# Audio tower kernel: part of the attention beside the last scans, scans and loads reordered, unread products on TensorE

## The chip, the cores and the metric

The kernel runs on one NeuronCore of a Trainium2 chip. The core has five engines that each work through their own list of instructions in order and wait for each other through semaphores: PE (TensorE, matrix products), DVE (VectorE), ACT (ScalarE), POOL (GpSimd) and SP (SyncE, which here only issues DMA transfers). The metric is the device time of one launch in microseconds. The three timed runs of the kernel before took 843.44, 845.51 and 848.17 us, median 845.51 us. The profiled execution took 837.19 us, of which its span is 835.0 us.

## The reference, cut to what matters

The reference has three parts in a row: three state-space layers with a halving of the sequence between them (750, 375, 187 positions), an attention with polynomial features, and a mixture of 16 experts. All is in 32-bit floats.

```python
def _ssm_layer(x, A_log, Dp, W_dbc, W_dt, b_dt):
    A = -jnp.exp(A_log)
    dbc = jnp.einsum('ble,ce->blc', x, W_dbc)
    delta, Bm, Cm = jnp.split(dbc, [DT_RANK, DT_RANK + N_STATE], axis=-1)
    delta = jax.nn.softplus(jnp.einsum('blr,er->ble', delta, W_dt) + b_dt)
    dA = jnp.exp(delta[..., None] * A)
    dBx = (delta * x)[..., None] * Bm[:, :, None, :]
    _, hs = jax.lax.associative_scan(combine, (dA, dBx), axis=1)
    return jnp.einsum('blen,bln->ble', hs, Cm) + Dp * x
# between layers: x.reshape(b, l // 2, 2, d).mean(axis=2)

h = h + attention(_layernorm(h))   # qkv, q and k divided by their norms, products of features, y / y_norm, projection
h = h + ffn(_layernorm(h))         # gate, softmax, the best 2 of 16 experts, silu(h1) * h2, w3
```

## The kernel before, in words

The batch of 32 is laid out as 2 groups of 64 channels on 128 partitions, 16 sequences in a row on the free axis. The scans are cut into 28 *units*: 16 of 750 columns for the first layer, 8 for the second and 4 for the third. Units are gathered in eight *phases* (`PHASES`: six of 4 units, then two of 2; `UB` holds where each begins). `LAST` is 26, the first unit of the last phase; unit 27 (`LAST + 1`) ends the scans. For each phase a short chain of dependent steps decides from the extremes of the step sizes which of the 64 states are slow: `extremes`, `extremes_of_row`, `lowest`, `bounds`, `smallest_delta`, `exponents`, `classes`, `ranked_and_quadratic`, `picks`. The two slowest states (`STATIC`) are scanned one by one; the others decay at once and are done by a product of the matrices (`mixed`, `product`, `summed`, `by_delta`, `output`). If a phase has more slow states, `more_slots` loops over them; with this data the loops are branched over.

For one unit n the work is this.

- PE: `rows` makes the rows of C and of the step size; `mixed` and `summed` serve the fast states; `weighted_b(n, j)` makes the input of scan j; `sums(n, part)` adds neighbouring positions for the next layer.
- SP: `spread_rows` takes these rows through a buffer in DRAM and spreads each over 64 partitions (`St`, the step size, and `Ct`, C). `EVENTS` lists which rows belong together: event k holds C of one unit and the step size of the unit two later; `ROWS` says in which period each is made.
- ACT: `softplus` (the step size), `decay` (the factors of the scan), `rows_out` and `sums_out` (copies out of PSUM).
- POOL: `softplus`, `inputs` (step size times x) and `add` (which puts the unit's result in its place).
- DVE: `load`, `recur` (the scan, 1.7 us for a unit), `read` for both states; `product`, `by_delta`, `output`.

Every engine has a function `period(n)` which writes its instructions out in a fixed order, and the periods -2 to 27 follow one another. Nothing else sets the order: an instruction that waits holds up all that is behind it on its engine. In period n DVE scans unit n and prepares unit n + 1; PE prepares n + 1 and n + 2. `chain(n)` gives q, the place in a phase of four at which steps of the next phase's decision are woven in; `brief(n)` gives k = 0 and 1 for the periods 24 and 25, in which the last phase's decision is woven in between a phase of only two units; `straight(n)` marks the first decision, before any scan.

After the scans comes `attention()`, a pipeline over eight parts r of 376 columns (`QC`) in periods t. `stages(t)` gives the part that is in each stage: the first layernorm (`first_center`, `first_squares`, `first_variance`, `first_deviation`, `first_normalized`), then qkv and its norms (`project_qkv`, `qkv_bias`, `qk_squares`, `qk_sums`, `qk_norms`, `qk_scale`, `k_linear`, `q_linear`), then the features (`products`, eight multiplications each, on POOL for k and mostly for q, on DVE for q of part 0) and `moments`, `q_features`, `attend`, and so on. In the kernel before t = 0 and t = 1, in which only the first two stages have work, begin when unit 27 is done. Then `experts()` follows, bound by PE.

At the start SP loads x in seven parts (`X_PARTS`): four of one unit each, then three of 1500 KB. The 15 small weights of attention and experts (`later`) are issued in one go behind event 4.

## Time and profile before

| what | us |
|---|---|
| median of three timed runs | 845.51 |
| profiled execution | 837.19 |
| its span | 835.0 |
| start, to the first product of the scans at | 29.17 |
| scans end, first product of attention at | 370.06 |
| first `moments` product of attention at | 397.05 |
| experts, first product at | 559.17 |

The page's line of the clock over the span in 40 slices shows the two places at which TensorE was slow: `PEclk9989999999999997666999999999999999999999`. The line of GB/s below it shows the loads at the left. To read this table: what happens before 29 us is a serial chain; from there to 315 us DVE and PE are both busy in most slices, with a few lower ones among them; between 315 and 397 us, where the last phases are short and the attention starts, every engine waits for others; from 397 us on a pipeline runs evenly, and from 559 us on PE never waits.

### The profile page before, as it was taken

How to read it: one execution, taken by the hardware profiler on the slowest of the kernel's cores; microseconds unless marked ns; L12 is line 12 of the kernel's file. 1: busy time of each engine (PE TensorE's matmuls, PEld its weight loads, DVE VectorE, ACT ScalarE, POOL GpSimd, SP SyncE). 2: the span in 40 equal slices, each digit the busy share in tenths (PEclk: the TensorE clock that was granted, in tenths of full speed). 3: DMA queues.
4: the chain of work that ended last, by engine and by line, in shares of the span. 5: the costliest groups of instructions: out<-in, count | busy, mean ns of one | idle time of the engine just before them, and what ended most of it. 6: DMA issues, size and time to landing. Idle time of an engine off the chain costs nothing.

```text
span 835.0 us, 11071 instructions
## 1 busy us (share of the span) xinstructions
PE 728.1 (87%) x3474; PEld 360.5 (43%) x3474; DVE 549.6 (66%) x859; ACT 426.2 (51%) x761; POOL 440.1 (53%) x402
## 2 busy tenths in 40 slices
PE   5778898989899894745998888878999999999997
PEld 2334444545445452412776666742333333333332
DVE  3477899998889896475458888849354444454443
ACT  2767587868676873512354554443334433344332
POOL 1457668686868575723555555523344444443441
PEclk9989999999999997666999999999999999999999
DMA  3475443424344432132000000072584443444400
GB/s 129 139 225 154 105 120 91 133 80 113 94 114 112 112 96 76 37 88 52 2 1 1 3 3 4 3 147 59 122 178 95 90 88 85 89 100 99 105 1 19
DMA packets 29233, 70.19 MB, mean 84 GB/s; under 512 B 4387, under 2 KB 20079, under 8 KB 28527
## 3 DMA queue, kind: packets, MB, share of 16 engines
q1 hardware_dynamic: 28863, 68.77, 33.7%
q8 instruction: 31, 0.51, 0.3%
q10 hardware_dynamic: 304, 0.63, 0.2%
q14 instruction: 35, 0.29, 0.1%
HBM read 66.96 MB, written 2.43 MB: 83 GB/s over the span
## 4 chain that ended last, share of the span: by engine, by line
PE 44%; DVE 8%; ACT 2%; issue 1%; DVEq 0%; ACTq 0%
PE pair L818 21%; PE pair L839 11%; PE pair L721 4%; PE pair L704 3%; PE pair L753 2%; DVE big L1420 1%; PE pair L768 1%; PE pair L740 1%; PE pair L762 1%; PE pair L685 1%; DVE big L1425 0%; ACT big L1100 0%; DVE big L1438 0%; DVE big L1728 0%; DVE big L1475 0%
## 5 line engine op out<-in xcount | busy, mean ns | idle before, releaser
L1583 DVE TENSOR_TENSOR hidden<-pair,tmp 128x502 f32<-128x502 f32 (+1 forms) x192 | 121.6, 675 | 129.4 <-PE pair L818 104.9
L1702 POOL TENSOR_TENSOR hidden<-xs,big 128x502 f32<-128x502 f32 (+1 forms) x96 | 111.9, 1167 | 167.4 <-PE pair L818 146.8
L1153 ACT ACTIVATE tmp<-pair 128x502 f32<-128x502 f32 (+1 forms) x192 | 102.5, 586 | 157.2 <-PE pair L818 157.2
L1728 POOL TENSOR_TENSOR big<-big 94x512 f32<-94x512 f32 (+3 forms) x120 | 89.7, 781 | 78.0 <-DVE big L1485 71.2
L818 PE MATMUL pair<-xs,w 64*128 64x502 f32 (+1 forms) x384 | 107.4, 636 | 0.5 <-DVE big L1517 0.5
L818 PE MATMUL pair<-hidden,w 64*128 64x502 f32 (+1 forms) x384 | 98.3, 588 | 3.1 <-DVE hidden L1583 3.0
L1293 DVE TENSOR_TENSOR_SCAN pair<-tmp,pair 128x750 f32<-128x750 f32 (+1 forms) x56 | 95.9, 1713 | 0.3
L839 PE MATMUL pair<-hidden,w 128*64 128x502 f32 (+1 forms) x384 | 91.1, 596 | 0.0
L463 PE MATMUL pair<-big,work 128*128 128x512 f32 x112 | 65.6, 669 | 7.6 <-DVE work L1305 4.3
L1605 POOL TENSOR_TENSOR big<-big,work 128x750 f32<-128x750 f32 (+1 forms) x28 | 45.6, 1629 | 46.9 <-ACT big L896 46.6
L818 PEld LDWEIGHTS pair<-hidden,w 64*128 64x128 f32 x384 | 37.0, 188 | 49.8 <-issue 44.8
L818 PEld LDWEIGHTS pair<-xs,w 64*128 64x128 f32 x384 | 29.4, 186 | 67.3 <-issue 36.2
L1633 POOL TENSOR_TENSOR big<-big,work 128x375 f32<-128x375 f32 (+1 forms) x24 | 22.0, 917 | 66.9 <-ACT big L964 66.5
L1286 DVE TENSOR_TENSOR pair<-pair,big 128x750 f32<-128x750 f32 (+1 forms) x56 | 52.0, 929 | 5.5 <-PE pair L464 5.0
L913 ACT ACTIVATE tmp<-big,picked 128x749 f32<-128x749 f32 (+2 forms) x56 | 49.9, 910 | 7.5 <-POOL big L1610 5.3
L839 PEld LDWEIGHTS pair<-hidden,w 128*64 128x64 f32 x384 | 23.4, 136 | 61.9 <-DVE hidden L1583 34.8
L1615 POOL TENSOR_TENSOR big<-big 128x750 f32<-128x750 f32 (+1 forms) x28 | 46.7, 1667 | 2.2
L1610 POOL TENSOR_TENSOR big<-big,work 128x750 f32<-128x750 f32 (+1 forms) x28 | 46.2, 1650 | 2.2
L1608 POOL TENSOR_TENSOR work<-work 128x750 f32<-128x750 f32 (+1 forms) x28 | 46.1, 1648 | 1.3 <-ACT work L902 1.3
L721 PEld LDWEIGHTS pair<-big 93*120 93x120 f32 (+1 forms) x384 | 42.1, 184 | 2.6 <-issue 1.4
L721 PE MATMUL pair<-big 93*120 93x65 f32 (+1 forms) x384 | 42.6, 268 | 0.0
L1271 DVE TENSOR_TENSOR pair<-pair,big 128x750 f32<-128x750 f32 (+1 forms) x28 | 26.4, 944 | 22.3 <-PE pair L464 16.7
(185 smaller groups left out, 1281.4 us busy)
## 6 DMA issues: line engine op xcount, KB each, us to landing
big<-dispatched SPq DMA_DIRECT2D x40, 502.0 KB, 6.6
spread<-rowsd SPq DMA_DIRECT2D x48, 375.0 KB, 5.7
spread<-rowsd SPq DMA_DIRECT2D x48, 187.5 KB, 3.3
big<-in_x SPq DMA_DIRECT2D x3, 1500.0 KB, 9.3
big<-dispatched SPq DMA_DIRECT2D x8, 498.0 KB, 5.8
spread<-rowsd SPq DMA_DIRECT2D x8, 374.0 KB, 4.9
w<-in_w SPq DMA_DIRECT2D x5, 512.0 KB, 7.0
big<-in_x SPq DMA_DIRECT2D x4, 375.0 KB, 3.8
```

The costliest lines, as they stand in the source:

```text
L463: pe.matmul(dst[:, 0:512], lhsT, rhs[:, 0:512], start=True, stop=True)
L721: mm = pe.matmul(bank[4 + n % 2][0:FT, at:at + 65], kF[r % 2][0:rows, unit, FT * f:FT * f + FT], qkv[r % 2][0:rows, unit, 143:208], start= ...
L818: pe.matmul(dst[:, 0:hi - lo], weights[blk, HID * e:HID * e + HID], x[blk, :], start=True, stop=True)\
L839: mm = pe.matmul(bank[4][64 * b:64 * b + 64, 0:hi - lo], w3[:, e, :], hidT[(2 * expert + b) % 8][:, 0:hi - lo], start=(e == 0), stop=(e == ...
L913: act.activation(seqs(dA[j], l)[:, :, 1:], seqs(of(delta, n), l)[:, :, 1:], ACT.Exp, scale=picked[p % 2][:, j:j + 1]).then_inc(dk_a, 1)
L1153: act.activation(sT[i % 4][:, 0:w], bank[BANK1[i]][:, 0:w], ACT.Silu).then_inc(silu_a, 1)
L1286: v.tensor_tensor(bu, bu, of(u, n), ALU.mult).then_inc(bu_v, 1)
L1293: v.tensor_tensor_scan(h, dA[j][:, 0:w], h, 0.0, ALU.mult, ALU.add).then_inc(sc_v, 1)
L1583: v.tensor_tensor(hidT[i % 8][:, 0:hi - lo], bank[BANK2[i]][:, 0:hi - lo], sT[i % 4][:, 0:hi - lo], ALU.mult)\
L1615: pool.tensor_tensor(of(u, n), of(delta, n), x, ALU.mult).then_inc(u_g, 1)
L1702: pool.tensor_tensor(xw[e % 4][:, 0:hi - lo], xs[:, lo:hi], wx[:, e, 0:hi - lo], ALU.mult)\
L1728: ins = eng.tensor_tensor(dst[:, :, at:at + H * m].rearrange("p u (h d) -> p u h d", d=m), t[:, :, :, 0:m], t[:, :, :, k:D], ALU.mult)
```

## The change

Seven things are changed.

1. **Attention beside scans.** The first layernorm of part 0 and 1 and qkv with its norms of part 0 are put into the periods 26 and 27 (`LAST`, `LAST + 1`), and `attention()` starts with t = 2. The products of q of part 0 on DVE stand behind the four `qkv_bias` of part 1 and no longer ahead of them.
2. **Unread products.** `idle(count, w)` issues `count` products of w columns into a PSUM bank that nobody reads: 6 of 256 columns before anything is loaded, 19 of 128 in the first decision, 3 of 376 and 10 of 128 in the last decision, 4 of 376 right ahead of the first `moments`.
3. **Order on PE.** `summed(n + 1)` goes ahead of `sums(n - 1, 0)` and, in period 25, of `weighted_b`; at the end of a phase `mixed(n + 2)` goes ahead of `sums(n, 0)`; `quadratic` is cut off `ranks` and goes behind `mixed`.
4. **Order on DVE.** `product` goes ahead of `ranked_and_quadratic`; in period 26 `recur(n, 0)` goes ahead of `product`.
5. **Order on POOL.** In the first period of a phase (`new`) `add` and `more_slots` of the phase before go ahead of `inputs(n + 1)`; in period 24 `softplus(n + 1)` goes ahead of them.
6. **Rows.** The C rows of unit 25 are made in period 23 instead of 24, so that period 24 has only the rows of the last phase's step sizes. For unit 0 C is spread ahead of the step size.
7. **Loads.** x has 13 parts: the last two parts of 1500 KB are cut into eight of 375 KB, one behind each of the events 3 to 10; the 15 small weights follow one by one behind the events 11 to 25.

On VectorE, at the end of the scans, these rows stand in the kernel before (periods 26 and 27; `pair` and `work` with 748 columns are the unit's own, `94x...` and `128x376` are attention's):

```order
L1286 TENSOR_TENSOR pair1<-pair1,big 128x748
L1265 TENSOR_TENSOR work<-pair3,big 128x748
L1293 SCALAR_TENSOR_TENSOR pair1<-tmp,pair1 128x748
L1286 TENSOR_TENSOR pair2<-pair2,big 128x748
L1305 TENSOR_TENSOR tmp<-pair1,spread 128x748
L1271 TENSOR_TENSOR pair3<-pair3,big 128x748
L1293 SCALAR_TENSOR_TENSOR pair2<-tmp,pair2 128x748
L1278 SCALAR_TENSOR_TENSOR work<-pair3,packed,big 128x748
L1305 TENSOR_TENSOR tmp<-pair2,spread 128x748
L1286 TENSOR_TENSOR pair1<-pair1,big 128x748
L1293 SCALAR_TENSOR_TENSOR pair1<-tmp,pair1 128x748
```

In the changed kernel the part from `output(27)` on reads like this on VectorE:

```order
L1356 SCALAR_TENSOR_TENSOR work<-pair3,packed,big 128x748
L1539 TENSOR_TENSOR big<-pair0,big 128x376
L1383 TENSOR_TENSOR tmp<-pair2,spread 128x748
L1364 TENSOR_TENSOR pair1<-pair1,big 128x748
L1371 SCALAR_TENSOR_TENSOR pair1<-tmp,pair1 128x748
L1554 TENSOR_TENSOR big<-pair3,bqkv 94x6x64 x2
L1364 TENSOR_TENSOR pair2<-pair2,big 128x748
L1383 TENSOR_TENSOR work<-pair1,spread 128x748
L1554 TENSOR_TENSOR big<-pair3,bqkv 94x6x64 x2
L1371 SCALAR_TENSOR_TENSOR pair2<-tmp,pair2 128x748
L1383 TENSOR_TENSOR work<-pair2,spread 128x748
L1564 TENSOR_REDUCE big<-big 94x128
```

The normalization (L1539) and the four biases (L1554) have come in between the scans (L1371), and the norms of q and k (L1564) come ahead of the last addition.

On TensorE the two last periods of the scans hold this in the kernel before, from `summed(27)` to the end:

```order
L463 MATMUL pair3<-work,packed 128x512
L464 MATMUL pair3<-work,packed 128x236
L498 MATMUL pair0<-big,rowsel1 32x374 x2
L463 MATMUL pair1<-big,work 128x512
L464 MATMUL pair1<-big,work 128x236
L463 MATMUL pair2<-big,work 128x512
L464 MATMUL pair2<-big,work 128x236
```

In the changed kernel the same stretch of TensorE reads:

```order
L490 MATMUL pair3<-work,packed 128x512
L491 MATMUL pair3<-work,packed 128x236
L527 MATMUL pair0<-big,rowsel1 32x374 x2
L734 MATMUL pair0<-resid,centering 128x376
L746 MATMUL pair0<-big,averaging 128x376
L490 MATMUL pair1<-big,work 128x512
L491 MATMUL pair1<-big,work 128x236
L767 MATMUL pair3<-wqkv,big 94x384 x2
L490 MATMUL pair2<-big,work 128x512
L491 MATMUL pair2<-big,work 128x236
L767 MATMUL pair3<-wqkv,big 94x384 x2
```

Ahead of `weighted_b(27, 0)` (L490, pair1) there are now a centering and an averaging, each of which waits for ACT, and projections stand ahead of and behind `weighted_b(27, 1)` (pair2).

The core of the diff, of the list of the rows, the loads and the periods of each engine:

```diff
     ROWS[_n] = [(_n + 1, _n + 3 if _n + 3 < LAST else None)]
+    if _n == LAST - 3:
+        ROWS[_n].append((_n + 2, None))
     if _n == LAST - 2:
-        ROWS[_n].append((Z_OF + LAST, LAST + 1))
+        ROWS[_n] = [(Z_OF + LAST, LAST + 1)]
...
-                if k in (1, 2, 3):
-                    load(k + 3)
-                elif k == 4:
+                if k == 1:
+                    load(4)
+                elif 3 <= k < 11:
+                    load(k + 2)
+                elif k == 11:
                     sp.wait_ge(zeroed, 1)
-                    for dst, src in later:
-                        sp.dma_start(dst, src).then_inc(later_in, 16)
+                if 11 <= k < 11 + len(later):
+                    dst, src = later[k - 11]
+                    sp.dma_start(dst, src).then_inc(later_in, 16)
...
+            def idle(count, w=128, src=packed, at=7):
+                for _ in range(count):
+                    pe.matmul(bank[at][:, 0:w], src[:, 0:128], src[:, 0:w], start=True, stop=True)
...
                 for e in range(EVENT_AT[n], EVENT_AT[n + 1]):
                     rows(e)
-                if old is not None:
-                    sums(old, 0)
-                if k == 1:
-                    weighted_b(n + 1, 0)
                 if nxt and not new:
                     summed(n + 1)
+                if old is not None:
+                    sums(old, 0)
...
+                if n == LAST:
+                    pe.wait_ge(later_in, LATER)
+                    pe.wait_ge(rw_a, len(EVENTS))
+                    pe.wait_ge(xa_g, LAST)
+                    pe.wait_ge(more_g, MG[NP - 1])
+                    first_center(0)
+                    first_variance(0)
-                if nxt and q != 0 and k != 1:
+                if nxt and q != 0:
                     weighted_b(n + 1, 0)
+                if n == LAST:
+                    project_qkv(0, 0)
+                    project_qkv(0, 1)
+                elif n == LAST + 1:
+                    project_qkv(0, 2)
+                    project_qkv(0, 3)
+                    first_center(1)
+                    first_variance(1)
...
                 if k == 0:
+                    idle(3, QC, at=1)
                     extremes_row(NP - 1)
                 elif n + 2 < UNITS:
-                    if last_of(n) is not None:
-                        sums(n, 0)
                     mixed(n + 2)
+                if q == 1:
+                    quadratic(p)
                 if last_of(n) is not None:
+                    sums(n, 0)
...
+                if n == LAST:
+                    first_squares(0)
+                    first_deviation(0)
+                elif n == LAST + 1:
+                    qk_squares(0)
+                    first_squares(1)
+                    qk_norms(0)
+                    first_deviation(1)
+                    k_linear(0)
...
             def period(n):
-                if n > 0 and n >= LAST - 2:
+                new = n > 0 and last_of(n - 1) is not None
+                if n >= LAST - 1:
                     add(n - 1)
...
                     softplus(n + 1)
+                if n < LAST - 1 and new:
+                    add(n - 1)
+                    more_slots(last_of(n - 1))
+                if 0 <= n + 1 < UNITS:
                     inputs(n + 1)
```

## Rows read from the trace of the kernel before

**Rows 1.** Windows: stretch, its us, busy us (instructions) by engine, clock, DMA share, GB/s.
```profile
11.65:31.97 20.32, 13.04 (x45) 5.28 (x45) 2.86 (x12) 9.06 (x20) 6.30 (x4) 1.00 0.32 114
47.38:98.10 50.72, 44.16 (x161) 22.11 (x161) 39.75 (x49) 29.29 (x47) 30.63 (x23) 0.90 0.53 147
98.10:184.39 86.29, 79.63 (x322) 40.74 (x322) 79.41 (x97) 66.50 (x105) 65.71 (x49) 1.00 0.42 110
325.16:340.82 15.66, 10.21 (x25) 5.50 (x25) 9.90 (x18) 7.70 (x15) 7.22 (x5) 0.50 0.17 49
353.05:369.96 16.91, 8.11 (x20) 3.37 (x19) 16.27 (x15) 2.20 (x3) 7.39 (x5) 0.70 0.20 47
370.06:397.05 26.99, 15.25 (x24) 5.83 (x25) 11.47 (x22) 6.07 (x11) 6.85 (x12) 0.60 0.36 78
```

**Rows 2.** Timeline (start, us, engine, line, operation, [idle before <- releaser]), first decision.
```profile
19.18 1.01 ACT L888 ACTIVATE work<-spread,packed,wdtc 128x750 f32<-128x750 f32 x1 [3.43 <-DMA spread<-rowsd]
29.17 2.08 PE L463 MATMUL pair<-big,quad 128*128 128x512 f32 x2 [0.45 <-DVE picked L1259]
33.30 1.13 PE L463 MATMUL pair<-work,packed 128*128 128x512 f32 x2
```

**Rows 3.** Timeline of SP's DMA issues: first and last small weight, next rows.
```profile
62.43 0.59 SPq L412 DMA_DIRECT2D wqkv<-in_wqkv  x1
...
70.21 0.39 SPq L412 DMA_DIRECT2D w<-in_w  x1
70.71 1.19 SPq L382 DMA_DIRECT2D rowsd<-rows  x4
```

**Rows 4.** Timeline of VectorE: reads of C that waited, and what followed.
```profile
44.06 0.94 DVE L1305 TENSOR_TENSOR tmp<-pair,spread 128x750 f32<-128x750 f32 x1 [2.85 <-DMA spread<-rowsd]
...
82.48 0.94 DVE L1305 TENSOR_TENSOR work<-pair,spread 128x750 f32<-128x750 f32 x1 [3.89 <-DMA spread<-rowsd]
...
91.48 0.94 DVE L1265 TENSOR_TENSOR work<-pair,big 128x750 f32<-128x750 f32 x1 [2.87 <-PE pair L464]
```

**Rows 5.** Timeline of VectorE: waits for `summed` and `mixed` in an even phase.
```profile
171.72 0.95 DVE L1271 TENSOR_TENSOR pair<-pair,big 128x750 f32<-128x750 f32 x1 [0.62 <-PE pair L464]
...
177.77 0.94 DVE L1265 TENSOR_TENSOR work<-pair,big 128x750 f32<-128x750 f32 x1 [0.90 <-PE pair L464]
...
195.54 0.95 DVE L1271 TENSOR_TENSOR pair<-pair,big 128x750 f32<-128x750 f32 x1 [0.84 <-PE pair L464]
```

**Rows 6.** Timeline, period 16: GpSimd's `inputs`, VectorE's `extremes`.
```profile
225.42 1.78 POOL L1615 TENSOR_TENSOR big<-big 128x750 f32<-128x750 f32 x1
...
231.01 0.94 DVE L1227 TENSOR_REDUCE smx<-pair 128x1 f32<-128x750 f32 x1 [2.07 <-PE pair L483]
```

**Rows 7.** Timeline, periods 24 to 26: VectorE, SP and ScalarE.
```profile
322.12 0.95 DVE L1271 TENSOR_TENSOR pair<-pair,big 128x748 f32<-128x748 f32 x1 [5.63 <-POOL big L1610]
...
325.50 2.40 SPq L391 DMA_DIRECT2D spread<-rowsd  x4
...
329.44 1.01 ACT L888 ACTIVATE work<-spread,packed,wdtc 128x748 f32<-128x748 f32 x1 [6.83 <-DMA spread<-rowsd]
...
348.25 0.95 DVE L1271 TENSOR_TENSOR pair<-pair,big 128x748 f32<-128x748 f32 x1 [6.23 <-PE pair L464]
...
353.05 0.94 DVE L1265 TENSOR_TENSOR work<-pair,big 128x748 f32<-128x748 f32 x1 [1.85 <-PE pair L464]
```

**Rows 8.** Timeline of attention's start: projections, bias, norms, features of k and q.
```profile
375.71 5.43 PE L704 MATMUL pair<-wqkv,big 128*94 128x384 f32 x8 [1.87 <-DVE big L1450]
...
377.34 0.55 DVE L1465 TENSOR_TENSOR big<-pair,bqkv 94x384 f32<-94x384 f32 x1 [1.69 <-PE pair L704]
...
382.86 1.22 DVE L1475 TENSOR_REDUCE big<-big 94x128 f32<-94x1024 f32 x1 [1.12 <-ACT big L1074]
...
386.27 6.49 POOL L1728 TENSOR_TENSOR big<-big 94x512 f32<-94x512 f32 x8 [15.85 <-DVE big L1485]
...
391.40 3.70 DVE L1728 TENSOR_TENSOR big<-big 94x512 f32<-94x512 f32 x8
```

556 lines of the change are left out of this document (303 added, 253 removed).

## The prediction

> **What bounds the kernel now.** I read the busy shares and the clock over the span first, then windows by stage, then the timeline of the windows in which VectorE and TensorE both wait. The reader is to see three regimes in the windows [rows 1]. From 98 to 184 us two phases take 86.29 us, 43.15 us each; VectorE is busy for 79.41 us of them and TensorE for 79.63 us, at full clock. So an even phase is bound by both at once, and about 3.4 us per phase are waits of each for the other. The phase before it, from 47.38 to 98.10 us, has the same 161 TensorE and 49 VectorE instructions and takes 50.72 us: 7.6 us are lost there. Between 325 and 397 us nothing is bound by throughput: VectorE is busy for 9.90 of 15.66 us, then for 16.27 of 16.91 us at the very end of the scans, then for 11.47 of 26.99 us while the attention pipeline fills, and TensorE has its half clock (1.2 GHz) in all of the first and much of the last two. Behind 397 us the change moves nothing, so I carry that part over as it is.
>
> **The start.** The granted clock reads 1.00 there, but the durations don't: a product of 512 columns takes 2.08 us at 29.17 us and 1.13 us at 33.30 us [rows 2]. I believe the durations: TensorE works at half speed until about 32 us. It is busy for 13.04 us between 11.65 and 31.97 us [rows 1]; at full speed that is 6.5 us less. Most of the chain runs through it, but the step sizes that ScalarE waits for come by DMA at 19.18 us [rows 2], and the products behind the first copy lie beside that transfer. I count 40% of the 6.5 us: 2.5 us. It needs the unread products to raise the clock. If they don't, 19 of them of 128 columns at half speed cost about 0.45 us each (four of 384 columns take 5.43 us [rows 8], one 1.36 us, a third of that), 8.6 us, of which the chain's own waits cover about three quarters: 2 us lost. Range -2 to +5.
>
> **Loads and rows of the first phase.** The 15 small weights keep SP from 62.43 to 70.21 us; the rows of the next event, which queue behind them, go out at 70.71 us [rows 3]. VectorE then waits 3.89 us for C at 82.48 us, and 2.87 us at 91.48 us [rows 4]. One by one they cost SP about 0.6 us per event, in an idle queue. At 44.06 us VectorE waits 2.85 us for C of unit 0, which lands behind the row of another unit and beside a load of 1500 KB; both are out of its way now. In the sum: the phase loses its excess of 7.6 us and the first read most of 2.85 us; I take 8.5 us, since some of both is the ordinary dip of the clock at a phase's start. Range 5 to 10.
>
> The Trainium skill ("DMA: Bandwidth & Descriptors", Bandwidth) speaks against cutting the loads of x: it wants transfers of 1 MiB or more, and gives about 2 us of fixed cost for each. By that page six more transfers would cost about 12 us if all of it were exposed, an estimate. The trace doesn't show such exposure: it shows the rows waiting in the queue behind others, which the cut relieves.
>
> **Order in the even phases.** Waits of VectorE that the new order is aimed at are 0.62 us for `summed` at 171.72 us, 0.90 us for `mixed` behind `sums(n, 0)` at 177.77 us and 0.84 us at 195.54 us [rows 5], some 2.7 us per phase with the smaller ones. `summed` takes nothing from `sums` but its place, so what waited for `sums` becomes late: `weighted_b(n + 1, 0)` ends 1.4 us later, and VectorE reads it some 3 us after its present end. That hides it. But TensorE is busy for 92% itself, so it gives back at most the same 3.4 us and rather less. I take 1 us for each of six phases, 6 us; range 0 to 14.
>
> In periods 16 and 20 the extremes of the next phase need the last unit of the phase before, which GpSimd adds only behind `inputs` of 1.78 us; VectorE waits 2.07 us at 231.01 us [rows 6]. With `add` ahead each loses about 1.5 us: 3 us in sum. What is late next is `inputs(n + 1)`, which `load(n + 1, 0)` reads only in the next period. Range 1 to 3.6.
>
> **Last decision.** At 322.12 us VectorE has waited 5.63 us for GpSimd's softplus of unit 25, which stood behind an addition that itself waited for sums [rows 7]. With softplus ahead it ends about 4.5 us sooner. But the decision also needs the step sizes of unit 26: the rows' copy into DRAM came beside a spread of C, so SP could go on only at 325.50 us, and ScalarE started at 329.44 us [rows 7]. C is now spread a period earlier. Against that, the addition now behind softplus is what the rows of unit 26 wait for, some 1.8 us later than before. I get 2.8 us. Range 0 to 5.6, the wait itself. TensorE is busy for 10.21 of 15.66 us there, all at half clock [rows 1]; full clock would give up to 4 us more. The unread products stand in gaps, but behind them TensorE still waits for ScalarE and the DMA; I count nothing.
>
> **Periods 25 and 26.** `by_delta(26)` waits 6.23 us, for `summed` behind `weighted_b`; with these swapped it waits 1.6 us less at half clock. `product(27)` waits 1.85 us ahead of the scan at 353.05 us [rows 7]; the scan now goes first and covers it. Together 3 us, since the later `weighted_b` takes some back. Range 1 to 6.
>
> **Attention beside the scans.** Work now on the path ahead of the last addition: five short VectorE operations of 0.55 us and the reduction of 1.22 us [rows 8] with a small one behind it (estimate 0.3 us), 4.3 us. VectorE has only 0.6 us of idle in that window [rows 1], so nothing hides them. The normalization waits for centering, square, averaging and two ScalarE steps that start behind the rows' copy: 0.4 to 2 us, and behind it `read(26, 1)` and all of unit 27 queue. In sum 6 us (4.7 to 7).
>
> Before, 26.99 us lay between the first centering and the first moments [rows 1]. Now, from the last addition: the two scale steps, 1 us, then 6.49 us of k's features on GpSimd [rows 8]: 7.5 us. TensorE starts the projections of part 1 when the second normalization is done, at about 2.3 us (estimate from the short operations), and takes 5.43 us at half clock [rows 8]: 7.8 us. Behind them stand four unread products of 376 columns, 2.5 us at full and 5 us at half clock: 10.3 to 12.8 us, take 11.5. They lie bare on the path, since the features are ready. VectorE's 3.70 us of q's features [rows 8] come before the moments are there. So 27.0 - 11.5 = 15.5 us gained, 6 us paid: 9.5 us. Range 4 to 13.
>
> **Sum.** 2.5 + 8.5 + 6 + 3 + 2.8 + 3 + 9.5 = 35.3 us. Against the profiled execution of 837.2 us that gives 801.9 us. The median of the timed runs, 845.5 us, lies 8.3 us above that execution; on it I forecast 845.5 - 35.3 = 810 us. All times below are on the median.
>
> **Rivals.**
> - *The clock doesn't follow, and the overlap is paid in the scans.* The unread products are too few where the chain waits for a DMA, the start costs 2 us, and VectorE, full in the last scans, hands back attention's gain but 4 us. For it: 16.27 of 16.91 us busy [rows 1]. Against it: the fill's 27 us are mostly latency, which overlap removes whatever VectorE does. Gain 35.3 - 4.5 - 5.5 = 25.3 us: 820 us.
> - *All terms near their upper bounds.* Full clock through the last decision (+4), the start at 5 (+2.5), an even phase at 2 us (+6): 48 us, 798 us. The Trainium skill ("TensorE: Matmul & The Clock Gate", Part 1) says that the slow clock is the default and activity releases it; the slow stretches with long waits agree [rows 1].
> - *The cut loads hold up the rows: slower.* Eight loads of x now go between the rows of periods 0 to 7. If each made the next C late as the block of small weights did, by 3.89 us [rows 4], that would be 31 us, and the 8.5 us of the first phase would not come: 845.5 - 26.8 + 31.1 = 850 us. It turns slower from 3.4 us per load (26.8 / 8). Against it: each has a quarter of the bytes of the load beside which 2.85 us were lost, and the queue is idle behind it.
> - *The change doesn't do what it says.* The order in the even phases gives nothing, because TensorE is as full as VectorE, and the loads give only the 3.89 us: 35.3 - 6 - 4.6 = 24.7 us, 821 us.
>
> **Chances.** Forecast (804 to 816) 0.46; the two rivals near 820 together 0.34; upper bounds 0.13; loads slower 0.03; a smaller gain than all of these, or none, 0.04. A difference under 0.5% (4.2 us) can't be told from none. The range goes from 798 to 829 us: it takes in both rivals near 820 with 9 us for the other end of their terms, and leaves out the slower case. Faster 0.94, same 0.03, slower 0.03.
>
> **What would show it.** In the new profile: no wait of VectorE over 1.5 us for a spread row before 100 us, and the phase from the first chain's end to the next near 43 us; L463's likes of 512 columns at about 1.1 us in the first decision; the wait of 5.63 us gone and ScalarE's softplus of unit 26 about 3 us sooner against period 23; from the last addition to the first moments 10 to 13 us, with four unread products right ahead of them; last two periods longer by 5 to 7 us. Wrong would be: the even phase longer than 43.15 us, VectorE waiting for the first normalization by more than 2 us, or a clock of 0.50 during the first 30 us' durations.

## The result, and the profile after

The changed kernel takes 813.66 us (four executions, 809.96 to 814.64), the kernel before 844.48 us in the same comparison: ratio 0.963, 95% interval 0.957 to 0.970. The profiled execution took 809.96 us, its span is 807.7 us. Measured again on another chip (ratio 0.965, 0.958 to 0.971), the ten executions together have the median 812.8 us and reach from 809.1 to 818.3 us. I compare the experiments with 812.8 us; the kernel before had medians from 844.5 to 846.7 us in the comparisons, and 848.6 us when it was measured once more by itself (e9). The ratios leave out executions more than 1.5% above the quickest of the same kernel; the medians given here hold all. With a spread of 9 us within one kernel, a difference of 2 us between medians is not told from none, and there the traces have to speak.

The same stretches as [rows 1], from the windows of the changed kernel (VectorE's last addition, which ends the scans, ends at 357.46 us), and as a last row the pipeline from the first moments to the fifteenth:

```profile
11.28:31.86 20.58, 17.29 (x83) 9.98 (x83) 2.86 (x12) 9.06 (x20) 6.30 (x4) 0.68 0.33 113
45.61:90.72 45.11, 42.68 (x161) 21.52 (x161) 39.83 (x50) 32.06 (x52) 32.10 (x24) 0.92 0.52 135
90.72:178.30 87.58, 79.57 (x322) 40.82 (x322) 79.89 (x97) 66.32 (x105) 66.11 (x49) 1.00 0.50 127
310.81:326.90 16.09, 12.86 (x46) 8.13 (x44) 8.36 (x18) 7.81 (x15) 8.04 (x5) 0.71 0.17 49
340.47:357.46 16.99, 9.10 (x26) 3.92 (x24) 15.49 (x19) 5.91 (x11) 6.42 (x8) 0.97 0.21 47
357.46:366.82 9.36, 6.80 (x17) 3.42 (x18) 6.19 (x13) 3.19 (x5) 5.93 (x8) 0.69 0.88 193
369.49:509.50 140.01, 126.84 (x1005) 99.15 (x1005) 102.43 (x204) 67.25 (x149) 83.14 (x112) 0.98 0.01 2
```

The first phase is 5.6 us shorter (45.11 against 50.72), the two even phases are 1.3 us *longer* (87.58 against 86.29), and the 27 us between the scans' end and the first moments have become 9.4. How far the trace of after runs ahead of that of before, mark by mark:

| mark (start of) | before | after | ahead |
|---|---|---|---|
| first copy of the picks (DVE) | 28.8 | 28.3 | 0.4 |
| extremes, first phase of scans | 47.4 | 45.6 | 1.8 |
| extremes, next | 98.1 | 90.7 | 7.4 |
| after two even phases | 184.4 | 178.3 | 6.1 |
| period 16 | 231.0 | 221.1 | 9.9 |
| period 20 | 275.0 | 263.8 | 11.1 |
| last decision begins | 324.6 | 308.7 | 15.9 |
| its picks | 340.8 | 326.9 | 13.9 |
| first moments copied (DVE) | 399.7 | 369.5 | 30.2 |
| last moments of the pipeline | 540.9 | 513.4 | 27.5 |
| span | 835.0 | 807.7 | 27.3 |

So the two profiles show 27.3 us of gain, while the medians show 31 to 34. Experiment e9 is about that gap.

### The profile page after: what moved, and what is told of

Read it like the earlier page. It is cut to its first block, busy times and chain, and to the rows that moved or that the text cites. A ratio compares the mean times of both kernels' runs of the same rounds, so it can differ in the third digit from the quotient of the medians.

```text
span 807.7 us, 11253 instructions
## 1 busy us (share of the span) xinstructions
PE 734.1 (91%) x3558; PEld 371.6 (46%) x3558; DVE 547.7 (68%) x859; ACT 425.0 (53%) x761; POOL 439.3 (54%) x403
## 4 chain that ended last, share of the span: by engine, by line
PE 46%; DVE 8%; ACT 2%; issue 1%; DVEq 0%; ACTq 0%
PE pair L882 22%; PE pair L903 11%; PE pair L784 4%; PE pair L816 3%; PE pair L767 2%; PE pair L831 1%; PE pair L803 1%; DVE big L1510 1%; PE pair L825 1%; ACT big L1174 1%; DVE big L1515 1%; DVE big L1517 0%; DVE big L1574 0%; DVE big L1575 0%; DVE big L1564 0%
## 5 line engine op out<-in xcount | busy, mean ns | idle before, releaser
L1371 DVE TENSOR_TENSOR_SCAN pair<-tmp,pair 128x750 f32<-128x750 f32 (+1 forms) x56 | 96.0, 1714 | 0.4
L1695 POOL TENSOR_TENSOR big<-big,work 128x750 f32<-128x750 f32 (+1 forms) x28 | 45.6, 1628 | 52.2 <-ACT big L962 52.2
L490 PE MATMUL pair<-big,work 128*128 128x512 f32 x112 | 61.7, 633 | 1.7 <-DVE work L1383 1.6
L1364 DVE TENSOR_TENSOR pair<-pair,big 128x750 f32<-128x750 f32 (+1 forms) x56 | 52.2, 931 | 2.5 <-PE pair L491 1.7
L979 ACT ACTIVATE tmp<-big,picked 128x749 f32<-128x749 f32 (+2 forms) x56 | 49.6, 909 | 2.5 <-issue 1.7
L490 PE MATMUL pair<-big,quad 128*128 128x512 f32 x56 | 32.6, 666 | 11.2 <-DVE work L1356 10.6
L784 PE MATMUL pair<-big 93*120 93x65 f32 (+1 forms) x384 | 42.6, 268 | 0.0
```

What stands on the lines that cost most here:

```text
L490: pe.matmul(dst[:, 0:512], lhsT, rhs[:, 0:512], start=True, stop=True)
L784: mm = pe.matmul(bank[4 + n % 2][0:FT, at:at + 65], kF[r % 2][0:rows, unit, FT * f:FT * f + FT], qkv[r % 2][0:rows, unit, 143:208], start= ...
L979: act.activation(seqs(dA[j], l)[:, :, 1:], seqs(of(delta, n), l)[:, :, 1:], ACT.Exp, scale=picked[p % 2][:, j:j + 1]).then_inc(dk_a, 1)
L1364: v.tensor_tensor(bu, bu, of(u, n), ALU.mult).then_inc(bu_v, 1)
L1371: v.tensor_tensor_scan(h, dA[j][:, 0:w], h, 0.0, ALU.mult, ALU.add).then_inc(sc_v, 1)
```

## The experiments

The diffs are from the changed kernel, with - for its lines, and are cut to their core (`...`).

### e1: attention's first two stages behind the scans again

```diff
-                if n == LAST: ... first_center(0); first_variance(0); project_qkv(0, 0..1)
-                elif n == LAST + 1: ... project_qkv(0, 2..3); first_center(1); first_variance(1)
             def attention():
+                first_center(0); first_variance(0)
+                for i in range(4): project_qkv(0, i)
+                first_center(1); first_variance(1)
```

and likewise on ScalarE and VectorE. Only the place is undone: within the fill ScalarE's squares of part 1 still go ahead of its norms of part 0, and VectorE's products of q of part 0 behind the biases of part 1, as in the changed kernel.

> The changed kernel with attention's first two stages (first_center, first_variance, the four project_qkv, their squares, norms, biases and sums of half 0, and the centring of half 1) issued after the last add again, all else as changed. Theory (the traces: the work from the last add to the first moments shrank, 17.8 us of gain came between the end of the scans and the first moments, and about 5 us of it were paid inside periods 25 and 26): 9 to 14 us slower than the changed kernel, about 825 us, and the scans end about 5 us earlier than in the changed kernel, near 352.5 us instead of 357.5. Rival (the overlap only moved the wait: PE, ACT and POOL are full in these periods and the moments wait for POOL's features anyway): within 3 us of the changed kernel. Second rival (the overlap was free in the scans): the scans end within 1 us of the changed kernel's, and the time is 15 us or more longer.

Measured: 822.1 us, ratio 0.972 (0.969 to 0.976), 9.3 us slower. VectorE's last addition starts at 354.41 us and the wait for the first normalization is back:

```profile
354.41 0.94 DVE L1378 TENSOR_TENSOR resid<-resid,work 128x748 f32<-128x748 f32 x1
360.60 0.55 DVE L1514 TENSOR_TENSOR big<-pair,big 128x376 f32<-128x376 f32 x1 [5.25 <-ACT big L1111]
...
381.65 0.56 DVE L1560 TENSOR_TENSOR big<-pair,featw 120x384 f32<-120x384 f32 x1 [1.46 <-PE pair L766]
```

From the picks (328.5 us) to that addition it takes 25.9 us; in the changed kernel, from 326.9 to 356.60 us, 29.7. The overlap costs the scans 3.8 us and saves 14.4 behind them (27.2 us from the last addition to the first copy of the moments in e1, 12.9 in the changed kernel). The theory holds, with 3.8 us paid where it said 5; neither rival does.

### e2: loads of x and small weights as before

```diff
-                if k == 1: load(4)
-                elif 3 <= k < 11: load(k + 2)
-                if 11 <= k < 11 + len(later): ...one small weight
+                if k in (1, 2, 3): load(k + 3)
+                elif k == 4: ...all small weights
```

> The changed kernel with only the loads of x and of the later weights as before: three loads of 1500 KB in periods 1 to 3 and all small weights in one go behind event 4. The order of the rows within an event stays as changed. Theory (the first phase became 5.6 us shorter because SP issues fifteen small loads no longer ahead of rows that DVE reads): 4 to 6 us slower than the changed kernel, about 819 us, with DVE's reads near 82 and 91 us again waiting 3 to 4 us for C, and nothing different after 98 us beyond that delay. Rival (the gain came from the order of rows inside an event, C rows behind the z and step-size rows): within 1.5 us of the changed kernel. Rival (the small cuts of x cost something later, because each is an issue on SP): 2 us or less slower, since what the first phase loses comes back later.

Measured: 815.6 us, ratio 0.964 (0.961 to 0.967), 2.8 us slower. The first phase takes 51.6 us again (extremes at 46.3 and 98.0 us). SP's queue and VectorE's read in its trace:

```profile
63.06 0.59 SPq L430 DMA_DIRECT2D wqkv<-in_wqkv  x1
...
71.87 1.19 SPq L390 DMA_DIRECT2D rowsd<-rows  x4
```
```profile
83.42 0.94 DVE L1377 TENSOR_TENSOR work<-pair,spread 128x750 f32<-128x750 f32 x1 [4.75 <-DMA spread<-rowsd]
```

The wait of 3.89 us at [rows 4] is back as 4.75. Its trace is 4.8 to 6.2 us behind those of the changed kernel at the first moments (375.7 against 369.5 and 370.9 us) but only 2 to 4 us in the span (811.3 against 807.7 and 809.6; the second number of each pair is of e5, the changed kernel once more). The changed kernel's pipeline has short stretches at half clock, at 417 to 422 and 503 to 507 us, that this execution doesn't have. So the gain in the phase is shown, 6.5 us (51.6 against 45.1); how much of it arrives at the end is between the theory and the second rival, and from one trace I can't say that the give-back belongs to the change.

### e3: no unread products; e12: only those of the start and the first decision; e8: without the four ahead of the moments

```diff
# e3
-                for _ in range(count):
+                for _ in range(0):
# e12: idle(...) removed at k == 0, at k == 1 and at att == 0
# e8
-                        idle(4, QC)
```

> The changed kernel without any of the products that nobody reads (the memset and the wait ahead of the first ones stay); nothing of the result depends on them. Theory (they kept no clock where it mattered: the granted clock was 0.50 at 12 to 18 us, from 25.5 to 32 us and from 319 us in the last decision with them, while four of 376 columns lie bare ahead of the first moments for 2.7 us and three in the last decision delay the row of extremes by 1 to 2.5 us): 2 to 5 us faster than the changed kernel, about 810 us. Rival (they hold TensorE's clock in the decisions and in front of the moments: without them the last decision and the first moments run at 0.50): 3 to 8 us slower, with the mean granted clock over 300 to 370 us lower by 0.05 or more. Rival (both cancel): within 1.5 us.

> The changed kernel with the unread products of the start and of the first decision alone (six of 256 columns and nineteen of 128), without those of the last decision and those ahead of the first moments. Theory (in the first decision they lift the clock for some of its products at 19 to 25 us and the first copy of the picks comes 0.3 us earlier than without them; the others cost 2.8 us): 2 to 3.5 us faster than the changed kernel, about 809.5 us, within 1 us of the kernel without any. Rival (the half clock at 11 to 33 and 45 to 53 us, which the kernel without any doesn't show, is real and costs time): 1 to 2 us slower than without any.

> The changed kernel without the four unread products of 376 columns ahead of the first moments alone. Theory (they lie bare on the path, 2.69 us in the trace after; the kernel without any unread products reached the first moments 2.6 us earlier): 2 to 3 us faster than the changed kernel, and the first moments as much earlier. Rival (the clock would fall in the moments without them and take it back): within 1 us, with half clock after 367 us.

Measured: e3 810.0 us, ratio 0.958 (0.955 to 0.962); e12 810.6 us, 0.960 (0.956 to 0.964); e8 813.5 us, 0.966 (0.960 to 0.973). The ten executions of e3 and e12 lie at 808.4 to 812.4 us; seven of the ten of the changed kernel lie above 812.2. So the products cost 2 to 3 us together, and by the medians (0.6 us apart) those of the start neither give nor cost. In the traces the picks of the first decision are copied at 28.0 to 29.9 us in the ten with the products of the start and at 28.4 to 28.8 us in the four without. TensorE in the first decision, with them:

```profile
17.64 2.04 PE L487 MATMUL pair<-packed 128*128 128x128 f32 x12
19.61 0.38 PE L570 MATMUL pair<-packed,smx 128*1 128x128 f32 x2
...
28.24 1.22 PE L487 MATMUL pair<-packed 128*128 128x128 f32 x4
29.25 1.91 PE L490 MATMUL pair<-big,quad 128*128 128x512 f32 x2
```

and without (e3):

```profile
19.50 0.59 PE L570 MATMUL pair<-packed,smx 128*1 128x128 f32 x2 [1.13 <-DVE smx L1305]
...
29.02 2.07 PE L490 MATMUL pair<-big,quad 128*128 128x512 f32 x2 [0.45 <-DVE picked L1337]
```

They do lift the clock: the product for the row of extremes takes 0.38 us instead of 0.59. But it falls again before the large product comes, which takes 1.91 us, against 1.13 us at full clock [rows 2]. The first phase takes 45.1 us in e12 and in the changed kernel and 43.6 in e3; by the column of the clock TensorE is at half clock for 6.8 us of 45 to 55 us in these two and for 3.4 in e3. That this is the doing of the products isn't shown: of the kernels without any, the one before has 6.8 us there and e10 has 3.4.

In the last decision the three of 376 columns stand in front of the step that they were to serve:

```profile
310.11 3.06 PE L487 MATMUL pair<-packed 128*128 128x376 f32 x6
313.10 0.38 PE L570 MATMUL pair<-packed,smx 128*1 128x128 f32 x2
...
314.69 1.01 ACT L954 ACTIVATE work<-spread,packed,wdtc 128x748 f32<-128x748 f32 x1 [5.22 <-DMA spread<-rowsd]
...
318.54 0.30 PE L579 MATMUL pair<-packed,amax 128*64 128x128 f32 x1 [2.02 <-ACT amax L994]
...
320.08 1.22 PE L487 MATMUL pair<-packed 128*128 128x128 f32 x4
321.23 0.79 PE L589 MATMUL pair<-wCT,wBTf 64*128 64x128 f32 x2
322.53 2.08 PE L490 MATMUL pair<-big,quad 128*128 128x512 f32 x2 [0.50 <-DVE quad L1333]
```

and without them (e3):

```profile
315.72 1.01 ACT L954 ACTIVATE work<-spread,packed,wdtc 128x748 f32<-128x748 f32 x1 [5.53 <-DMA spread<-rowsd]
...
319.66 0.39 PE L579 MATMUL pair<-packed,amax 128*64 128x128 f32 x1 [4.36 <-ACT amax L994]
...
321.43 0.79 PE L589 MATMUL pair<-wCT,wBTf 64*128 64x128 f32 x2
```

The row of extremes starts 4.4 us behind VectorE's reduction (308.70 us), 1.6 us in e3 (309.43, 311.02). But this delay isn't on the path. ScalarE waits over 5 us for the spread row of step sizes with and without them, and TensorE's next step of the decision (L579), which follows ScalarE, starts 9.8 us behind the reduction in the changed kernel, 10.2 in e5 and 10.2 in e3. What does lie on the path are two products of 128 columns (1.22 us at half clock) behind it: L589 starts 2.7 us behind L579 with them (2.8 in e5) and 1.8 without. From extremes to picks it takes 18.2 and 18.7 us in the two traces of the changed kernel and 17.4 in e3.

The first copy of the moments on VectorE in e8, without the four products:

```profile
361.65 5.40 PE L767 MATMUL pair<-wqkv,big 128*94 128x384 f32 x8 [5.14 <-DVE big L1538]
...
366.85 5.39 PE L784 MATMUL pair<-big 94*120 94x65 f32 x47
...
367.57 3.07 DVE L1825 TENSOR_TENSOR big<-big 94x512 f32<-94x512 f32 x8
...
370.56 0.55 DVE L1584 TENSOR_TENSOR big<-pair,featw 120x384 f32<-120x384 f32 x1
```

In the changed kernel, and below it in e5, the same kernel once more:

```profile
360.02 4.43 PE L767 MATMUL pair<-wqkv,big 128*94 128x384 f32 x8 [5.14 <-DVE big L1539]
...
364.29 2.69 PE L487 MATMUL pair<-packed 128*128 128x376 f32 x8
...
369.49 0.56 DVE L1585 TENSOR_TENSOR big<-pair,featw 120x384 f32<-120x384 f32 x1 [1.45 <-PE pair L784]
```
```profile
360.40 5.40 PE L767 MATMUL pair<-wqkv,big 128*94 128x384 f32 x8 [5.23 <-DVE big L1539]
...
365.60 2.78 PE L487 MATMUL pair<-packed 128*128 128x376 f32 x8
...
370.89 0.56 DVE L1585 TENSOR_TENSOR big<-pair,featw 120x384 f32<-120x384 f32 x1 [1.50 <-PE pair L784]
```

The four take 2.6 to 2.8 us, but only 1.5 to 1.6 us of it is on the path: from the start of the projections to the first copy of the moments it takes 10.5 us in e5 and 8.9 in e8, whose projections are as slow, and 9.5 us in the changed kernel and 7.9 in e12, whose projections are both quick (4.43 us). With the four, VectorE waits 1.50 us (1.45 in the changed kernel) for the moments behind its 3.07 us of products for q's features. Without them the moments start sooner, and VectorE comes to copy them with no wait left: it is now its own products that end last. The clock doesn't explain e8: the projections stand ahead of the four in the program, and they take 5.40 us with (e5) as without (e8); behind 366.85 us TensorE is back at full clock within 0.7 us. So the theory for e8 holds in kind and fell in size, and its rival, the clock, isn't seen. The median of e8, 0.7 us above that of the changed kernel, doesn't resolve 1.5 us.

### e4: the order in the long phases as before

```diff
-                if nxt and not new: summed(n + 1)
                 if old is not None: sums(old, 0)
+                if nxt and not new: summed(n + 1)
...
+                    if last_of(n) is not None: sums(n, 0)
                     mixed(n + 2)
-                if q == 1: quadratic(p)
-                if last_of(n) is not None: sums(n, 0)
```

with `quadratic` behind `ranks`, and `ranked_and_quadratic` ahead of `product` on VectorE.

> The changed kernel with TensorE's and VectorE's order in the long phases as before: the sums of the unit before ahead of the summed C of the next, the quadratic form straight behind the ranks, the last unit's first sums ahead of the mixing, and VectorE's step for ranks ahead of the product. Theory of the prediction (1 us a phase, six phases): 4 to 8 us slower than the changed kernel, about 820 us. Theory that the traces of both kernels suggest (the even phases from 98 to 184 us took 86.3 us before and 87.6 after, since by_delta now waits for POOL, with 0.6 to 1.2 us a time, so that the order is not what limits them): within 2 us of the changed kernel, either side. Rival (the order is worse with the rest of the change): 2 to 4 us faster.

Measured: 813.7 us, ratio 0.962 (0.958 to 0.965), 0.9 us slower. What VectorE waits for in the two even phases (us in total, times, longest), first the changed kernel, then e4:

```profile
DVE pair L1349 <- POOL big L1700: 2.3, 2, 1.2
DVE work L1383 <- DMA spread<-rowsd: 2.1, 2, 1.3
DVE pair L1349 <- PE pair L491: 1.6, 2, 0.8
DVE work L1343 <- PE pair L491: 1.3, 4, 0.3
```
```profile
DVE work L1345 <- PE pair L491: 4.9, 4, 1.6
DVE pair L1351 <- PE pair L491: 3.5, 6, 0.8
DVE pair L1366 <- PE pair L491: 1.2, 2, 0.7
```

The waits for TensorE go from 9.6 to 2.9 us, but GpSimd's step size and the spread rows take 4.4 us in their place. VectorE has no wait for GpSimd at that operation (L1351) in e4, from 90 to 320 us; in the changed kernel it has six there (L1349), 4.9 us in total. The two phases take 89.0 us in e4, 87.6 and 88.2 in the two traces of the changed kernel. In the kernel before these waits for TensorE came to 4.6 us and the phases to 86.3; e4 has half clock at 93 to 98, 138 to 142 and 182 to 186 us, the kernel before had none there. So a good part of the 9.6 us is clock, and e4 doesn't price the order alone: from the extremes to the next reduction of the chain (`lowest`) it takes 6.7 us in e4 and 5.1 in both other kernels. What brings those stretches is open.

### e6: GpSimd's add behind `inputs` again

```diff
-                if n < LAST - 1 and new:
+                if n == LAST - 2 and new:
                     add(n - 1)
```

and in the other new periods behind `inputs`.

> The changed kernel with GpSimd's add of the unit before behind inputs of the next unit again in the first period of each phase (period 24, next to the last decision, stays as changed). Theory of the prediction (the summed x of a unit that the next phase's products wait for comes later): periods 16 and 20 become 1.5 us longer each, the time 2 to 4 us. Theory from the trace after (by_delta now waits 0.6 to 1.2 us for GpSimd's softplus in the even phases): the wait comes from the changed place of the add, and without it the time is 1 to 3 us shorter. Rival: the two cancel, within 1 us.

Measured: 815.9 us, ratio 0.965 (0.958 to 0.972), 3.1 us slower in the median (2.4 without the longest of the six executions, 822.1 us), which alone is not told from none. Its trace has the wait of [rows 6] again, and 1.23 us at the next such place (272.18 us):

```profile
226.72 0.94 DVE L1305 TENSOR_REDUCE smx<-pair 128x1 f32<-128x750 f32 x1 [2.70 <-PE pair L512]
```

The phases that end there take 45.9 and 45.5 us, in the two traces of the changed kernel 42.8 to 43.6. That is more than the waits; half clock at 225 to 232 and 272 to 277 us is in it. The theory that the add causes the new waits for GpSimd falls: from 90 to 320 us VectorE waits for it 5.0 us in e6, in seven waits, and 4.9 in the changed kernel, in six. With e4, which has none, they come with the new order.

### e7: the last decision's preparations as before

```diff
-    if _n == LAST - 3: ROWS[_n].append((_n + 2, None))
-        ROWS[_n] = [(Z_OF + LAST, LAST + 1)]
+        ROWS[_n].append((Z_OF + LAST, LAST + 1))
-                if n >= LAST - 1:  (GpSimd: add ahead of softplus)
+                if n >= LAST - 2:
```

> The changed kernel with the last decision's preparations as before: C rows of unit 24 and the z and step-size rows of units 25 and 26 issued in one period (two events in period 23), and GpSimd's add ahead of the softplus in period 24. Theory (the wait of 5.6 us for those rows is gone in the trace after, and phase 5's last stretch, 264 to 309 us, is 4.8 us shorter than before, of which the clock, at half for 275 to 279 us before, is about 1): 3 to 5 us slower than the changed kernel. Rival of the prediction's own term (2.8 us). Rival (all of it was the rows' loads and the order, not this part): within 1 us.

Measured: 818.1 us, ratio 0.969 (0.963 to 0.975), 5.3 us slower. VectorE's timeline has a wait of 6.83 us for GpSimd in e7, first below. In the changed kernel, second, it waits 1.09 us for TensorE at that operation.

```profile
315.60 0.95 DVE L1347 TENSOR_TENSOR pair<-pair,big 128x748 f32<-128x748 f32 x1 [6.83 <-POOL big L1698]
```
```profile
305.81 0.95 DVE L1349 TENSOR_TENSOR pair<-pair,big 128x748 f32<-128x748 f32 x1 [1.09 <-PE pair L491]
...
308.70 0.55 DVE L1305 TENSOR_REDUCE smx<-pair 128x1 f32<-128x374 f32 x1 [0.33 <-ACT rows L1023]
```

The phase up to the last decision takes 50.4 us in e7, 44.9 and 44.6 in the two traces of the changed kernel. The decision itself is 1.3 to 1.8 us shorter in e7 (16.9 against 18.2 and 18.7 us): what was moved ahead is partly waited for behind, as the prediction said. So the traces give about 4 us and the medians 5.3. The experiment undoes the rows and GpSimd's order together and doesn't say which gave how much.

### e11: two places in periods 25 and 26 as before

```diff
+                if k == 1: weighted_b(n + 1, 0)
                 if nxt and not new: summed(n + 1)
...
-                if n in (0, LAST): recur(n, 0)
+                if n == 0: recur(n, 0)
```

> The changed kernel with two places of the last periods as before: in period 25 weighted_b of unit 26 ahead of the summed C on TensorE, and in period 26 the scan behind the product on VectorE. Theory of the prediction (1.6 us less of waiting at by_delta and 1.85 us at the product): 2 to 4 us slower than the changed kernel, about 816 us, and by_delta of unit 26 waits 6 us again. Rival (the first normalization sits behind the same operations and takes it back): within 1 us.

Measured: 814.0 us, ratio 0.964 (0.960 to 0.969), 1.2 us slower, and from picks to first moments 42.6 us, as in the changed kernel. `by_delta` of unit 26 waits as long with the old order, first row below, as with the new, second row (VectorE's timeline of each):

```profile
335.93 0.95 DVE L1351 TENSOR_TENSOR pair<-pair,big 128x748 f32<-128x748 f32 x1 [4.71 <-PE pair L491]
```
```profile
332.73 0.95 DVE L1349 TENSOR_TENSOR pair<-pair,big 128x748 f32<-128x748 f32 x1 [4.63 <-PE pair L491]
```

The rival holds. What went from 6.23 us [rows 7] to 4.63 is not the order's doing; TensorE came back to full clock at about 333 us in the changed kernel and 334 in e11, and only behind 348 us before, which no run tests by itself. The other place is real but small: VectorE waits 0.71 us at the product ahead of the scan in e11 (339.59 us) and not at all in the changed kernel.

### e5, e9, e10: both kernels again, and the overlap alone

e5 is the changed kernel, e9 the kernel before, e10 the kernel before with attention's first stages in periods 26 and 27 and only what goes with them (the projections of part 0 have PSUM banks of their own, and the features of q and k have changed places in memory, as in the changed kernel):

```diff
# e10, from the kernel before
+                if n == LAST: ... first_center(0); first_variance(0); project_qkv(0, 0..1)
+                elif n == LAST + 1: ... project_qkv(0, 2..3); first_center(1); first_variance(1)
```

> The changed kernel itself, once more, on the chip of the runs that it is compared with. If what the profiles show is what the medians show, its median stands near that of the kernel without the order change (813.7 us) plus or minus 1.5 us, and 3 to 4 us above that of the kernel without unread products (810.0 us). Rival: its time varies with where TensorE's half clock falls, and its median lies at 810 us or below; then the unread products cost nothing and the order gives 3 us.

> The kernel before itself, once more. Its timed executions so far lie mostly at 843 to 848 us with a mean granted clock of 0.931 to 0.941, while the one whose profile the prediction was read from took 837.2 us at 0.953. Theory (the trace used for the sum was an unusually quick execution, and a part of what the change gains on the median is half clock that this trace doesn't show): if this profile is of an ordinary execution, it has 10 to 18 us more of half clock than the first one, in places at which TensorE waits, most likely in the first phase or from 324 to 397 us. Rival (the additional half clock lies in the experts' part behind 559 us or in the pipeline, which the change doesn't touch): then the change's gain on the median is not explained by it.

> The kernel before with attention's first two stages beside the last scans, and nothing else of the change: no unread products, loads, rows and the order on each engine as before. Theory (the parts add up, and undoing this one in the changed kernel cost 8 to 10 us): 8 to 11 us faster than the kernel before. Rival (in the kernel before more of TensorE's half clock lies in the filling of the attention, 27 us in its trace, so that removing it gives more there than in the changed kernel): 13 to 18 us faster. Rival (it needs the other changes, because VectorE in period 27 waits for the product ahead of the scan): 5 us or less.

Measured: e5 812.5 us, as its theory said: 2.5 us above e3. e9 848.6 us in the median of 12 executions (833.7 to 851.1), its profiled one with a span of 848.3 us: nine of the twelve took 846 us or more, the other three 833.7 to 841.6. e10 830.5 us, ratio 0.982 (0.978 to 0.987), 15 to 16 us faster than the kernel before. In e9's trace these windows stand out:

```profile
21.00:35.00 14.00, 9.65 (x28) 4.92 (x29) 2.47 (x9) 8.02 (x21) 6.31 (x4) 0.51 0.40 134
82.00:90.00 8.00, 5.40 (x9) 2.58 (x9) 6.09 (x6) 3.98 (x7) 0.00 (x0) 0.57 0.58 147
229.00:237.00 8.00, 6.78 (x25) 2.93 (x26) 3.72 (x6) 4.56 (x6) 6.27 (x5) 0.57 0.57 149
389.00:418.00 29.00, 22.79 (x95) 17.19 (x96) 12.42 (x24) 6.75 (x13) 10.96 (x13) 0.53 0.00 1
406.60:549.80 143.20, 129.99 (x1005) 102.78 (x1005) 102.51 (x204) 67.31 (x149) 83.13 (x112) 0.95 0.01 3
```

and the pipeline's stretch in the first trace of the kernel before:

```profile
399.70:537.10 137.40, 123.73 (x1005) 97.31 (x1005) 102.52 (x205) 67.15 (x149) 82.16 (x110) 1.00 0.01 3
```

The same 1005 products take 143.2 us instead of 137.4, because the half clock of the attention's start runs on into the pipeline until 418 us. These 5.8 us are the largest piece of the 13.3 us between the two spans of one kernel; the rest has gathered before it (e9 is 1.4 us behind at 98 us, 2.3 at 275, 3.6 at 325 and 6.9 at the first moments). By the mean clock (0.927 of 848.3 us against 0.953 of 835.0) e9 was at half clock for 45 us more, of which the 14 at the start are only a matter of the column (below). That is more than my 10 to 18, and its main place is one that I had given to the rival. That the quick execution hid half clock is shown. That all of it is where TensorE waits is not. The changed kernel's two traces have full clock in the pipeline but for 4 to 5 us at a time.

e10's rival with 13 to 18 us holds in size: from picks to first moments it takes 44.8 us, e9 62.0.

## Why the prediction was right, point by point

The forecast of 810 us with 798 to 829 was near the 813.7 us measured, and faster was right. On the traces it was not as near: the sum of 35.3 us was read from an execution of 837.2 us and gives 801.9, and the profiled execution of the changed kernel took 810.0, a gain of 27.3 us in the span. The sum was not right in its parts either. What each was worth when undone by itself:

| term of the sum | predicted | undone, on the median | trace |
|---|---|---|---|
| start, unread products | 2.5 | 0 (e12 to e3) | 0.4 sooner, within the spread |
| loads and rows, first phase | 8.5 | 2.8 | 5.6 of the phase, 1.4 ahead of it |
| order in the even phases | 6 | 0.9 | 0.8 to 1.4 for two phases |
| GpSimd's add | 3 | 3.1 | waits of 2.70 and 1.23 back |
| last decision | 2.8 | 5.3 | about 4; wait of 6.83 back |
| periods 25 and 26 | 3 | 1.2 | wait unchanged |
| overlap | 9.5 | 9.3 | 14.4 saved, 3.8 paid; the order in the fill not undone |
| unread products behind the start | in the overlap | -2.2 (e12) | 0.9 to 1.0 and 1.5 to 1.6 lost |
| sum | 35.3 | 20.4 | |

- **What bounds it** was read rightly for the even phases: both engines full. From this "it gives back at most the same 3.4 us" followed, and then I took 1 us a phase. That was the mis-sized term. The waits aimed at did shrink (to 2.9 us for two phases, from 4.6 in the kernel before and 9.6 in e4 with its half clock), but GpSimd's softplus was the next to be late, although GpSimd is busy for only three quarters of the time, and nobody in the prediction was named as next there. The phase "longer than 43.15 us", which the prediction gave as a sign of being wrong, came: 43.8.
- **The start.** The step "it needs the unread products to raise the clock" was right and "40% of 6.5 us" was not: the clock rose for the short products and fell before the long one (1.91 us, where the prediction's sign was 1.1). The traces give this term nothing.
- **First phase.** The mechanism is shown by e2. The size of 8.5 us was 7.0 in the trace. The rule of the Trainium skill ("DMA: Bandwidth & Descriptors", Bandwidth) to batch transfers to 1 MiB or more, which speaks against cutting the loads of x, did not decide here: the phase with the cut loads takes 45.11 us and the one of e2, with the large ones, 51.6. The figures in that section are of transfers issued from GpSimd, and this kernel issues from SyncE; the fixed cost of about 2 us that the prediction gives stands on that page in another section (Anatomy of one DMA — SWDGE (gpsimd) path), for GpSimd as well. e2 puts the small weights back as well, so that it doesn't price the size of a load alone.
- **Last decision.** The mechanism is right, and the term was half of what undoing it costs. I had set the later rows of unit 26 against 4.5 us of gain; against e7 they cost 1.3 to 1.8 us, and the wait that went was 6.8 us. From the kernel before to the changed one the traces give just the 2.8 us: the phase up to the decision is 4.8 us shorter (44.9 against 49.6) and the decision 2.0 longer (18.2 against 16.2), to which the unread products add 0.9 to 1.0.
- **Periods 25 and 26.** The step failed. The wait isn't set by what stood ahead of `summed`: e11 has it at 4.71 us with the old order and the changed kernel at 4.63. That the 1.6 us to the 6.23 of before are TensorE's clock is likely from when it came back, and not shown. Of the 1.85 us at the product, e11 shows 0.71.
- **Overlap.** Paid: 6 us said, 3.8 measured. VectorE is busy for 3.7 us more between picks and last addition (23.22 against 19.51 in e1), so the new work was paid in full, but was 3.7 and not 4.3 us, and the 1.24 us for which it waits for the first normalization stand against 1.09 us of waiting for a spread row in e1. Gained: 15.5 us said, 14.4 measured against e1, 17.6 against the kernel before (26.99 less 9.36). From the last addition to the moments 9.4 us were measured, 11.5 said, since the projections took 4.43 us and not 5.43; in e5, where they took 5.40, it is 10.5 us.
- **The four products "lie bare on the path"**: 2.6 to 2.8 us long, as said, but only 1.5 to 1.6 us of it is bare. The prediction had VectorE's products for q's features end before the moments are there; without the four they end last.
- **The slower rival** didn't come: the cut loads make no read of C wait more than 0.82 us before 100 us (1.71 in e5, just over the 1.5 that the prediction had set as a sign).

Why did a sum with 20.4 us in its parts come out near the measured 31 to 34? The overlap is worth 9.3 us when taken from the changed kernel and 15 to 16 when given to the kernel before. These 6 to 7 us are part of the missing 10 to 14, and a part of them e1 can't show, because it leaves the new order within the fill in place. The second normalization, first in the trace of the kernel before, then in e1:

```profile
390.94 0.55 DVE L1450 TENSOR_TENSOR big<-pair,big 128x376 f32<-128x376 f32 x1 [4.02 <-ACT big L1057]
```
```profile
371.55 0.55 DVE L1514 TENSOR_TENSOR big<-pair,big 128x376 f32<-128x376 f32 x1
```

It comes 15.8 us behind the first (375.11 us) in the kernel before, where ScalarE does its squares only at 387.54 us behind the linear features, and 11.0 behind it (360.60 us) in e1. Behind it VectorE goes on with 3.70 us of products of q [rows 8] in the kernel before, and the biases wait for them. From the last addition to the first copy of the moments it takes 30.7 us in the kernel before and 27.2 in e1, which has the four unread products in it. Another part is half clock: in e9 the same stretch takes 33.3 us. How the rest divides I haven't measured: no run undid two parts at once. So the forecast was right partly by luck: terms too large for order, start and periods 25 and 26 stood in for gains that the single experiments don't show.

The kernel without any unread products (e3) is the quickest measured, 810.0 us, ahead of both kernels.

## What to carry to other kernels

When two engines are both full in a stage, look up which engine ends next after the wait that a better order removes, and give the term no more than the difference to that one; here the wait moved to the third engine. A chain of short products with waits on other engines was not kept at full clock by a few filler products. A filler costs what it takes only where nothing else is late: here three products of 376 columns cost nothing beside ScalarE's wait for a DMA, two of 128 were paid almost in full, and of four of 376 a little more than half. The same reading tells what to expect from taking one out. Take a sum from a trace whose execution is an ordinary one: here the first trace was 8 us below the median, and the largest piece of its distance to an ordinary one was half clock in a part that the change seemed not to touch.

## What the hardware showed that I had not expected

- The clock's column can read 1.00 at the start although TensorE is slow. For 21 to 35 us the first trace of the kernel before reads 1.00 and that of e9 reads 0.51, with 9.38 and 9.65 us of TensorE busy and the picks copied at 28.8 and 28.4 us. In e3 the column reads 1.00 too and the product of 512 columns takes 2.07 us. From 33 us on column and durations agree in both (1.13 and 1.12 us for such a product).
- Half clock can stay through busy work: in e9 from 389 to 418 us, the last 11 us of them in the pipeline, where TensorE is busy for nine tenths (10.34 of 11 us, clock 0.54).
- Ten executions of one binary differ by 9 us (809.1 to 818.3), with a mean granted clock of 0.970 in the quickest and 0.956 in the slowest.
- Fifteen small issues on SP cost 0.4 to 1.1 us each, 8.8 us from the first to the next rows (63.06 to 71.87 us in e2), and VectorE waits 4.75 us for what stands behind them.
